# Two large graph aggregations: waits placed on small memsets instead of register operations, sizes loaded as 16-bit values, the last one's tiles in a loop

## The chip, the core and the metric

The kernel runs on one core of a Trainium2 chip. The metric is the device time of one execution in microseconds. Engines: PE (TensorE), DVE (VectorE), ACT (ScalarE), POOL (GpSimd) and SP (SyncE).
## The reference

Two graph layers, each followed by a mixture of experts, on 6250 nodes of 256 features. The change touches the two full-width graph attention layers, which compute for each node d over its edges (s, d), some 206250 of them:

```python
e = leaky_relu(e_left[src] + e_right[dst], 0.2)
e_exp = exp(e - segment_max(e, dst)[dst])
alpha = e_exp / (segment_sum(e_exp, dst)[dst] + EPS)
out = segment_sum(Wh[src] * alpha[:, :, None], dst)
```

The first layer has 8 heads of 32 channels, the last 4 heads of 64 (with roles of source and destination swapped and no self loops). Between them stands a small attention layer of 4 heads of 4 channels, which has a function of its own (`aggregate_small`) and is not touched.

## The kernel before

Edges are sorted by destination on the chip and nodes ranked by degree, so that 128 nodes with similar degrees form a tile (NT = 49 tiles). A list gives each of the 128 partitions its neighbours, slot by slot. `aggregate` runs one large aggregation; it is called twice, for the first layer (with 8 heads, and `beside` holding pieces of the sorting of the other two lists, which DVE, PE and ACT do between tiles) and for the last (4 heads, nothing beside).

- **POOL** (`Stream.gpsimd`, L902 to L915) gathers rows of the table by indirect DMA, one slot of 128 rows per instruction (L914), into a ring of 96 slots. It waits at L906 on `taken`, which DVE raises, before it overwrites ring entries of 16 slots.
- **SP** (`Stream.sync`) waits for gathers, raises `ready` and loads index lists.
- **ACT** (`lay`, L1129 to L1148) waits for `ready`, copies the scores' left parts out of the ring into `el` in groups of 16 slots (L1142) and blanks the edges of the chunk (L1145, L1146); `tile` (L1151) takes the exponential (L1155) and lays the next chunk, and stores the tile's result (L1127).
- **DVE** (`tile`, L1047 to L1109) does the rest. A tile's slots are cut into chunks of up to 64 slots; here nearly every tile is one chunk. Per chunk it makes the scores and the running maximum (L1055 to L1067), waits for the exponential, multiplies the tail's eight slots into `wide` (L1070, recorded at L1042), and then runs a register loop over units of eight slots (L1075): product into `part` (recorded at L1042), sum into `wide` (L1080). It folds `wide` and adds it to `acc` (L1081 to L1095). At a tile's end it divides and writes `res` (L1100 to L1108).

Sizes of a tile (number of slots per chunk, chunks, first slot, first chunk) stand in `sizes` and are loaded into registers by L1006. The loops over chunks and units are loops of the sequencer; the loop over tiles is written out 49 times.
## Time and profile before

| | us |
|---|---|
| median of three runs (lowest, highest) | 10115.43 (10109.69, 10125.95) |
| span of the profiled execution | 10110.4 |
| DVE busy | 5594.3 (55%) |
| POOL busy | 5337.1 (53%) |
| PE busy | 2288.8 (23%) |
| ACT busy | 1093.7 (11%) |

The profiled execution's own time is its span. Register, branch, wait and DMA-issuing instructions are not counted as busy; where they are shown they carry a q after the engine's name (DVEq). In a timeline a row gives the start, the duration, the engine, the line and in brackets the engine's idle time before it and what ended it; "issue" is time for which the profile knows no other cause. In a group row the numbers are busy time in all, the mean duration of one in ns, and the idle time before them with its releasers. The first large aggregation lies between about 1063 and 3690 us, the last between about 6383 and 8751 us.

### The profile page before, as it was taken

How to read it: one execution, taken by the hardware profiler on the slowest of the kernel's cores; microseconds unless marked ns; L12 is line 12 of the kernel's file. 1: busy time of each engine (PE TensorE's matmuls, PEld its weight loads, DVE VectorE, ACT ScalarE, POOL GpSimd, SP SyncE). 2: the span in 40 equal slices, each digit the busy share in tenths (PEclk: the TensorE clock that was granted, in tenths of full speed). 3: DMA queues.
4: the chain of work that ended last, by engine and by line, in shares of the span. 5: the costliest groups of instructions: out<-in, count | busy, mean ns of one | idle time of the engine just before them, and what ended most of it. 6: DMA issues, size and time to landing. Idle time of an engine off the chain costs nothing. (4 is left out here: it accounts for less than half of the span.)

```text
span 10110.4 us, 54577 instructions
## 1 busy us (share of the span) xinstructions
PE 2288.8 (23%) x9111; PEld 1752.0 (17%) x9112; DVE 5594.3 (55%) x8828; ACT 1093.7 (11%) x2533; POOL 5337.1 (53%) x5411
## 2 busy tenths in 40 slices
PE   2112000000000002146555512000000000129995
PEld 1111000000000001135444411000000000116663
DVE  8764588788777677523333275455656556421111
ACT  1101000000000001112222201000000000002221
POOL 0025656666676654455555345776666777542221
PEclk7555555555555555578777755555555555559997
DMA  4051333433333353411111162433333333620004
GB/s 142 22 159 50 97 82 87 122 99 98 101 101 98 102 113 74 122 23 33 29 28 28 30 172 89 109 100 92 101 98 101 106 99 99 129 97 30 30 30 117
DMA packets 458121, 869.43 MB, mean 86 GB/s; under 512 B 175134, under 2 KB 294860, under 8 KB 448192
## 3 DMA queue, kind: packets, MB, share of 16 engines
q0 software_dynamic: 239536, 575.99, 23.0%
q1 hardware_dynamic: 167648, 182.04, 6.2%
q10 hardware_dynamic: 50788, 110.02, 3.3%
q14 instruction: 129, 1.06, 0.0%
q8 instruction: 20, 0.33, 0.0%
HBM read 693.35 MB, written 180.71 MB: 86 GB/s over the span
## 5 line engine op out<-in xcount | busy, mean ns | idle before, releaser
L914 POOL DMA_INDIRECT agg_ring<-table,agg_idx x4320 | 4275.8, 990 | 2329.8 <-issue 1323.4
L1042 DVE TENSOR_TENSOR agg_part<-agg_ring,agg_prob 128x2048 f32 x420 | 964.4, 2296 | 631.8 <-issue 556.2
L1080 DVE TENSOR_TENSOR agg_wide<-agg_wide,agg_part 128x2048 f32<-128x2048 f32 x420 | 960.4, 2287 | 14.4
L1786 PE MATMUL dense_tp<-all_ident,dense_xn 128*128 128x128 f32 x100 | 23.9, 425 | 2570.3 <-issue 2543.7
L1408 PE MATMUL agg_hp<-agg_xt,agg_w 128*128 128x256 f32 x1600 | 446.4, 439 | 579.4 <-ACT agg_ht L1378 340.3
L2208 DVE TENSOR_TENSOR experts_h<-experts_sg,experts_hp 128x682 f32<-128x682 f32 x106 | 91.8, 866 | 779.7 <-ACT experts_sg L2191 779.7
L2158 PE MATMUL experts_hp<-mixture_w,experts_xt 128*128 x1696 | 518.2, 458 | 0.6 <-ACT experts_xt L2187 0.6
L1408 PEld LDWEIGHTS agg_hp<-agg_xt,agg_w 128*128 128x128 f32 x1600 | 352.4, 224 | 663.8 <-ACT agg_ht L1378 360.4
L1786 PEld LDWEIGHTS dense_tp<-all_ident,dense_xn 128*128 128x128 f32 x100 | 20.3, 228 | 2571.9 <-issue 2544.5
L2129 POOL DMA_INDIRECT yc<-experts_ysb,experts_list x105 | 103.7, 987 | 685.2 <-DVE experts_ysb L2217 685.2
L1422 PE MATMUL agg_yp<-agg_w,agg_ht 128*128 128x256 f32 x1600 | 405.3, 411 | 231.0 <-remote 174.5
L1422 PEld LDWEIGHTS agg_yp<-agg_w,agg_ht 128*128 128x128 f32 x1600 | 330.4, 208 | 297.1 <-issue 246.9
L1042 DVE TENSOR_TENSOR agg_wide<-agg_ring,agg_prob 128x2048 f32 x98 | 224.2, 2288 | 275.0 <-issue 198.8
L488 POOL IOTA rank_thresholds<- 128x50 int32 x3 | 0.5, 170 | 686.4 <-POOLq L75 686.4
L2158 PEld LDWEIGHTS experts_hp<-mixture_w,experts_xt 128*128 128x128 f32 x1696 | 314.4, 190 | 174.6 <-issue 30.0
L217 PE MATMUL agg_words_turned<-all_ident,last_sort_words 128*128 128x128 f32 x48 | 10.9, 416 | 1454.1 <-issue 1454.1
L2179 PE MATMUL experts_yp<-mixture_w,experts_ht 128*128 x1260 | 309.4, 387 | 0.0
L1155 ACT ACTIVATE agg_prob<-agg_score 128x648 f32<-128x648 f32 (+1 forms) x98 | 56.7, 579 | 2332.1 <-issue 1387.9
L1055 DVE TENSOR_TENSOR agg_score<-agg_el,agg_er 128x640 f32<-128x640 f32 (+1 forms) x98 | 64.6, 659 | 410.0 <-issue 372.4
L514 POOL DMA_INDIRECT rank_start_g<-starts,rank_node_i x147 | 143.3, 975 | 225.9 <-DVE rank_degt L625 182.0
L217 PEld LDWEIGHTS agg_words_turned<-all_ident,last_sort_words 128*128 128x128 f32 x48 | 8.8, 216 | 1456.4 <-issue 1456.0
L522 POOL DMA_INDIRECT rank_wide<-copies,rank_widx x147 | 148.9, 1013 | 195.6 <-DVE rank_widx L679 154.8
(421 smaller groups left out, 6520.8 us busy)
## 6 DMA issues: line engine op xcount, KB each, us to landing
agg_ring<-table,agg_idx POOLq DMA_INDIRECT x4320
y<-agg_ysb ACTq DMA_DIRECT2D x25, 1024.0 KB
rank_y<-y SPq DMA_DIRECT2D x10, 2560.0 KB
rank_x<-x SPq DMA_DIRECT2D x30, 640.0 KB
copies<-first_sort_words SPq DMA_DIRECT2D x16, 1024.0 KB
copies<-last_sort_words ACTq DMA_DIRECT2D x16, 1024.0 KB
x<-rank_x SPq DMA_DIRECT2D x20, 640.0 KB
agg<-agg_res ACTq DMA_DIRECT2D x98, 128.0 KB
```

The costliest lines, as they stand in the source:

```text
L514: pool.indirect_dma_start(out=start_g[:, t:t + 1], out_offset=None, in_=starts.rearrange("(n a) -> n a", a=1), in_offset=bass.IndirectOffs ...
L522: pool.indirect_dma_start(out=wide[g % 2][:, u * ROW:(u + 1) * ROW], out_offset=None, in_=copies.rearrange("c (r w) -> (c r) w", w=ROW), i ...
L914: pool.indirect_dma_start(out=self.ring[:, to:to + self.RW], out_offset=None, in_=self.table, in_offset=bass.IndirectOffsetOnAxis(ap=index ...
L1042: return dve.tensor_tensor(to[:, :].rearrange("p (j h c) -> p j h c", j=UNIT, h=H), ring[:, ds(st.at(at_u), UNIT * RW)].rearrange("p (j w) ...
L1055: dve.tensor_tensor(sc3, el3, er[:, H:2 * H].unsqueeze(1).to_broadcast([P, SC // H, H]), ALU.add).then_inc(added, 1)
L1080: dve.tensor_tensor(wide[:, :], wide[:, :], part[:, :], ALU.add).then_inc(widened, 1)
L1408: mm = pe.matmul(self.hp[:, h:h + 2 * P], self.w1[:, at:at + P], xt3[:, :, k * P:(k + 1) * P], start=(k == 0), stop=(k == 1))
L1422: mm = pe.matmul(y, self.ht[:, n * 2 * P + u * P:n * 2 * P + (u + 1) * P], self.w2[:, n * D:(n + 1) * D], start=(c == 0), stop=(c == 3))
L2129: pool.indirect_dma_start(out=yc, in_=ysb[t % B][:, :], in_offset=None, out_offset=bass.IndirectOffsetOnAxis(ap=lst[:, t * 4 + 1:t * 4 + 2 ...
L2158: mm = pe.matmul(hp3[:, c, 0:HC], xt[:, kc * P:(kc + 1) * P], rhs, start=(kc == 0), stop=(kc == 1))
L2179: mm = pe.matmul(yp[:, 0:D], ht[0:m, j * P:(j + 1) * P], w2[0:m, ds(e * W2 + j * D, D)], start=(j == 0), stop=(j == HJ - 1))
L2208: dve.tensor_tensor(h[:, :].rearrange("p (c n) -> p c n", c=2), sg[:, :].rearrange("p (c n) -> p c n", c=2), hp3[:, 2:4, 0:HC], ALU.mult). ...
```

## The change

In `aggregate` alone. On DVE the waits for the exponential, the tail, the previous sum, the end of a chunk and the store of the result each get a memset of one to seven elements behind them (`passed`), so that the memset carries the wait; on ACT small activations into `junk` take the waits for `ready` and `copied`. Addresses and bounds are computed ahead of the waits and kept (`snap`). The event instructions that raised `dve_passed` go. The first slot of a tile is held as two 16-bit values, high part and low four bits, and the load takes six 16-bit values instead of five 32-bit ones. The position in `prob` is counted from the even unit at or below the first (`even`). Shifts and masks are written as divisions and remainders. WIDE is 16, as SLOTS is, so the groups have the size they had. Where nothing stands beside the aggregation (the last one) DVE's tiles 1 to 48 are a loop of the sequencer instead of being written out.

```diff
--- before.py
+++ after.py
@@ -971,6 +971,10 @@
 EARLY = 112
 
 
+LOAD = 6
+WIDE = 16
+
+
 def aggregate(nc, cfg, H, C, table, info, ell, out, self_loop, S, beside):
 
 
@@ -979,33 +983,36 @@
     CW = H * C
     RW = CW + 2 * H
     UH, UC = UNIT * H, UNIT * CW
-    GH = SLOTS * H
-    SC = (CH // SLOTS + 1) * GH
+    GH = WIDE * H
+    SC = (CH // WIDE + 1) * GH
+    WU = WIDE // UNIT
     with Scope(nc, f"agg{cfg.name}", S["keep"]) as s:
         st = Stream(nc, s, cfg, RW, table, ell, info)
         ring, taken = st.ring, st.taken
-        sizes = s.sb("sizes", [1, 5 * (NT + 1)], I32)
+        sizes = s.sb("sizes", [1, LOAD * (NT + 1)], mybir.dt.uint16)
+        bits = s.sb("bits", [1, 2 * (NT + 1)], I32)
...
         def sizes_of(eng, t):
             why = "the ranking bounds every size of a tile"
-            ng, nk, c0, k0, missing = nc.values_load_multi_w_load_instructions(sizes[0:1, ds(t * 5, 5)], engines=[eng.engine], min_val=0, max_val=cfg.max_slots,
-                                                                      skip_runtime_bounds_check_because=why)[1]
-            return nc.s_assert_within(ng, 1, CH, skip_runtime_bounds_check_because=why), nk, c0, k0, missing
+            ng, nk, c_high, c_low, k0, missing = nc.values_load_multi_w_load_instructions(
+                sizes[0:1, ds(t * LOAD, LOAD)], engines=[eng.engine], min_val=0, max_val=cfg.max_slots, skip_runtime_bounds_check_because=why)[1]
+            return nc.s_assert_within(ng, 1, CH, skip_runtime_bounds_check_because=why), nk, c_high * SLOTS + c_low, k0, missing
 
...
@@ -1025,32 +1032,39 @@
                 dve.wait_ge(st.info_in, 16)
-                of_tile = sizes[:, :].rearrange("p (t w) -> p t w", w=5)
+                of_tile = sizes[:, :].rearrange("p (t w) -> p t w", w=LOAD)
+                bits2 = bits[:, :].rearrange("p (t w) -> p t w", w=2)
+                dve.tensor_scalar(bits2[:, :, 0], st.inf[:, I_C0:I_C0 + NT + 1], 4, None, ALU.logical_shift_right).then_inc(halved, 1)
+                dve.tensor_scalar(bits2[:, :, 1], st.inf[:, I_C0:I_C0 + NT + 1], SLOTS - 1, None, ALU.bitwise_and).then_inc(halved, 1)
                 dve.tensor_scalar(of_tile[:, :, 0], st.inf[:, I_NG:I_NG + NT + 1], 1.0, None, ALU.max).then_inc(sized, 1)
-                dve.tensor_scalar(of_tile[:, :, 4], st.inf[:, I_NK:I_NK + NT + 1], -1.0, 4096.0, ALU.mult, ALU.add).then_inc(sized, 1)
-                for w, first in ((1, I_NK), (2, I_C0), (3, I_K0)):
-                    dve.tensor_copy(of_tile[:, :, w], st.inf[:, first:first + NT + 1]).then_inc(sized, 1)
+                dve.tensor_copy(of_tile[:, :, 1], st.inf[:, I_NK:I_NK + NT + 1]).then_inc(sized, 1)
+                dve.tensor_copy(of_tile[:, :, 4], st.inf[:, I_K0:I_K0 + NT + 1]).then_inc(sized, 1)
+                dve.tensor_scalar(of_tile[:, :, 5], st.inf[:, I_NK:I_NK + NT + 1], -1.0, 4096.0, ALU.mult, ALU.add).then_inc(sized, 1)
+                dve.wait_ge(halved, 2)
+                dve.tensor_copy(of_tile[:, :, 2:4], bits2[:, :, :]).then_inc(sized, 1)
                 dve.wait_ge(const, 5)
                 dve.wait_ge(sized, 5)
                 dve.sem_inc(taken, cfg.RU - 1)
                 dve.sem_inc(widened, cfg.RU)
                 acc3 = acc[:, :].rearrange("p (h c) -> p h c", h=H)
+                res3 = res[:, :].rearrange("p (h c) -> p h c", h=H)
                 sc3 = score[:, 0:SC].rearrange("p (j h) -> p j h", h=H)
                 el3 = el[:, GH:GH + SC].rearrange("p (j h) -> p j h", h=H)
 
-                def weigh(at_u, u, to):
-                    return dve.tensor_tensor(to[:, :].rearrange("p (j h c) -> p j h c", j=UNIT, h=H),
-                                             ring[:, ds(st.at(at_u), UNIT * RW)].rearrange("p (j w) -> p j w", w=RW)[:, :, 0:CW].rearrange("p j (h c) -> p j h c", h=H),
+                def weigh(at, to, u):
+                    return dve.tensor_tensor(to, ring[:, ds(at, UNIT * RW)].rearrange("p (j w) -> p j w", w=RW)[:, :, 0:CW].rearrange("p j (h c) -> p j h c", h=H),
                                              prob[:, ds(u * UH, UH)].rearrange("p (j h) -> p j h", h=H).unsqueeze(3).to_broadcast([P, UNIT, H, C]),
                                              ALU.mult)
 
-                def tile(t):
+                def tile(t, later):
                     ng, nk, c0, k0, _ = sizes_of(dve, t)
                     with dve.Fori(0, nk) as k:
-                        gg = c0 + k * ng
                         kk = dve.snap(k0 + k + 1)
-                        u0, u1 = gg >> 3, (gg + ng) >> 3
-                        nu = st.units(u1 - u0)
+                        gg = dve.snap(c0 + k * ng)
+                        u0, u1 = dve.snap(gg // UNIT), dve.snap((gg + ng) // UNIT)
+                        even = dve.snap(u0 // WU * WU)
+                        ending = dve.snap(st.at(u1))
+                        in_prob = nc.s_assert_within(u1 - even, 0, CU + WU - 2, skip_runtime_bounds_check_because="a chunk has 8 to 64 slots")
                         dve.wait_ge(laid, kk * 3)
                         dve.tensor_tensor(sc3, el3, er[:, H:2 * H].unsqueeze(1).to_broadcast([P, SC // H, H]), ALU.add).then_inc(added, 1)
                         dve.wait_ge(added, kk)
@@ -1066,16 +1080,16 @@
                         dve.wait_ge(kept, kk)
                         dve.tensor_tensor(sc3, sc3, mn[:, :].unsqueeze(1).to_broadcast([P, SC // H, H]), ALU.subtract).then_inc(scored, 1)
                         dve.wait_ge(probs, kk)
-                        first = u0 & 1
-                        weigh(u1, nu + first, wide).then_inc(tail, 1)
-                        n0 = dve.snap(u0 + cfg.RU)
-                        n1 = dve.snap(u1 + cfg.RU)
+                        dve.memset(passed[:, 5:6], 0.0)
+                        weigh(ending, wide[:, :].rearrange("p (j h c) -> p j h c", j=UNIT, h=H), in_prob).then_inc(tail, 1)
                         dve.wait_ge(tail, kk)
-                        dve.sem_inc(st.dve_passed, 1)
+                        dve.memset(passed[:, 0:1], 0.0)
+                        n0, n1 = dve.snap(u0 + cfg.RU), dve.snap(u1 + cfg.RU)
                         with dve.Fori(n0, n1) as n:
-                            u = nc.s_assert_within(n - n0, 0, CU - 2, skip_runtime_bounds_check_because="a chunk has 8 to 64 slots")
+                            u = nc.s_assert_within(n - even - cfg.RU, 0, CU - 1, skip_runtime_bounds_check_because="a chunk has 8 to 64 slots")
                             dve.wait_ge(widened, n)
-                            weigh(n, u + first, part).then_inc(taken, 1)
+                            dve.memset(passed[:, 6:7], 0.0)
+                            weigh(st.at(n), part[:, :].rearrange("p (j h c) -> p j h c", j=UNIT, h=H), u).then_inc(taken, 1)
                             dve.wait_ge(taken, n)
                             dve.tensor_tensor(wide[:, :], wide[:, :], part[:, :], ALU.add).then_inc(widened, 1)
                         dve.tensor_reduce(dsum[:, :], prob[:, 0:SC].rearrange("p (j h) -> p h j", h=H), AX.X, ALU.add).then_inc(totalled, 1)
@@ -1086,30 +1100,37 @@
                         dve.wait_ge(widened, n1)
                         dve.tensor_tensor(wide[:, 0:4 * CW], wide[:, 0:4 * CW], wide[:, 4 * CW:8 * CW], ALU.add).then_inc(quartered, 1)
                         dve.wait_ge(quartered, kk)
...
+                        dve.wait_ge(dens, kk)
+                        dve.memset(passed[:, 1:2], 0.0)
                         dve.wait_ge(combined, kk)
-                        dve.wait_ge(dens, kk)
-                        dve.sem_inc(st.dve_passed, 1)
-                    beside.vector(dve, t)
+                        dve.memset(passed[:, 2:3], 0.0)
+                    if beside.parts:
+                        beside.vector(dve, t)
                     dve.memset(m[:, :], NEG).then_inc(reset, 1)
                     dve.wait_ge(reset, t + 1)
                     dve.tensor_scalar(den[:, :], den[:, :], 1e-16, None, ALU.add if self_loop else ALU.max).then_inc(floored, 1)
                     dve.wait_ge(floored, t + 1)
-                    dve.reciprocal(den[:, :], den[:, :]).then_inc(inverted, 1)
-                    dve.wait_ge(inverted, t + 1)
-                    if t:
+                    dve.reciprocal(den[:, :], den[:, :]).then_inc(parts_done, 1)
+                    if later:
                         dve.wait_ge(out_stored, t * 16)
-                    dve.tensor_tensor(res[:, :].rearrange("p (h c) -> p h c", h=H), acc3,
-                                      den[:, :].unsqueeze(2).to_broadcast([P, H, C]), ALU.mult).then_inc(tile_done, 1)
-
-                for t in range(NT):
-                    tile(t)
+                        dve.memset(passed[:, 3:4], 0.0)
+                    dve.wait_ge(parts_done, t + 1)
+                    dve.tensor_tensor(res3, acc3, den[:, :].unsqueeze(2).to_broadcast([P, H, C]), ALU.mult).then_inc(tile_done, 1)
+
+                tile(0, False)
+                if beside.parts:
+                    for t in range(1, NT):
+                        tile(t, True)
+                else:
+                    with dve.Fori(1, NT) as t:
+                        tile(t, True)
 
             @block.tensor
             def _(pe):
@@ -1128,22 +1149,27 @@
 
                 def lay(t, fresh, k):
                     ng, nk, c0, k0, missing = sizes_of(act, t)
-                    gg = c0 + k * ng
+                    gg = act.snap(c0 + k * ng)
                     kk = k0 + k + 1
-                    g0, g1 = gg >> 4, (gg + ng) >> 4
-                    at = gg & (SLOTS - 1)
+                    g0, g1 = act.snap(gg // WIDE), act.snap((gg + ng) // WIDE)
+                    at = act.snap(gg % WIDE)
                     shown = at if self_loop else at + fresh
                     to = fresh * H
-                    act.wait_ge(st.ready, g1 + 1)
-                    act.activation(er[:, ds(to, H)], ring[:, ds((gg % cfg.RS) * RW + CW + H, H)], ACT.Copy).then_inc(laid, 1)
-                    act.activation(junk[:, :], zeros[:, 0:1], ACT.Exp)
-                    groups = nc.s_assert_within(g1 - g0 + 1, 1, CH // SLOTS + 1, skip_runtime_bounds_check_because="a chunk has up to 64 slots")
-                    with act.Fori(0, groups) as g:
-                        act.activation(el[:, ds((g + 1) * GH, GH)].rearrange("p (j h) -> p j h", h=H),
-                                       ring[:, ds(((g0 + g) % cfg.RING) * (SLOTS * RW), SLOTS * RW)].rearrange("p (j w) -> p j w", w=RW)[:, :, CW:CW + H], ACT.Copy).then_inc(copied, 1)
-                    act.wait_ge(copied, g1 + kk)
-                    act.activation(el[:, ds(shown * H, GH)], negs[:, 0:GH], ACT.Copy).then_inc(laid, 1)
-                    act.activation(el[:, ds((at + ng + SLOTS) * H, SC)], negs[:, :], ACT.Copy).then_inc(laid, 1)
+                    end = act.snap(g1 + 1)
+                    ready = act.snap(end * (WIDE // SLOTS))
+                    mine = act.snap((gg % cfg.RS) * RW + CW + H)
+                    act.wait_ge(st.ready, ready)
+                    act.activation(junk[:, 0:1], zeros[:, 0:1], ACT.Exp)
+                    act.activation(er[:, ds(to, H)], ring[:, ds(mine, H)], ACT.Copy).then_inc(laid, 1)
+                    with act.Fori(g0, end) as g:
+                        place = nc.s_assert_within(g - g0 + 1, 1, CH // WIDE + 1, skip_runtime_bounds_check_because="a chunk has up to 64 slots")
+                        act.activation(el[:, ds(place * GH, GH)].rearrange("p (j h) -> p j h", h=H),
+                                       ring[:, ds((g % (cfg.RS // WIDE)) * (WIDE * RW), WIDE * RW)].rearrange("p (j w) -> p j w", w=RW)[:, :, CW:CW + H], ACT.Copy).then_inc(copied, 1)
+                    before, behind, all_copied = act.snap(shown * H), act.snap((at + ng + WIDE) * H), act.snap(g1 + kk)
+                    act.wait_ge(copied, all_copied)
+                    act.activation(junk[0:1, 1:2], zeros[0:1, 0:1], ACT.Copy)
+                    act.activation(el[:, ds(before, GH)], negs[:, 0:GH], ACT.Copy).then_inc(laid, 1)
+                    act.activation(el[:, ds(behind, SC)], negs[:, :], ACT.Copy).then_inc(laid, 1)
 
                     return nk, k0, missing
 
@@ -1153,8 +1179,8 @@
                     with act.Fori(0, nk) as k:
                         act.wait_ge(scored, k0 + k + 1)
                         act.activation(prob[:, 0:SC + H], score[:, 0:SC + H], ACT.Exp).then_inc(probs, 1)
-                        fresh = act.snap(nc.s_assert_within((k + missing + 1) >> 12, 0, 1, skip_runtime_bounds_check_because="k is below the number of chunks"))
-                        following = lay(nc.s_assert_within(fresh + t, 0, NT, skip_runtime_bounds_check_because="the next tile"), fresh, (k + 1) * ((fresh + 1) & 1))
+                        fresh = act.snap(nc.s_assert_within((k + missing + 1) // 4096, 0, 1, skip_runtime_bounds_check_because="k is below the number of chunks"))
+                        following = lay(nc.s_assert_within(fresh + t, 0, NT, skip_runtime_bounds_check_because="the next tile"), fresh, (k + 1) * ((fresh + 1) % 2))
                     beside.scalar(nc, act, t)
                     return following
 
```

## Rows read from the trace of the kernel before

**Rows 1.** The page: busy us, share of the span, instructions of each engine.
```profile
PE 2288.8 (23%) x9111; PEld 1752.0 (17%) x9112; DVE 5594.3 (55%) x8828; ACT 1093.7 (11%) x2533; POOL 5337.1 (53%) x5411
```

**Rows 2.** Both stretches: span; PE, PEld, DVE, ACT, POOL busy; PE clock, DMA.
```profile
1120.00:3690.00 2570.00, 49.97 (x208) 39.87 (x208) 1971.59 (x2093) 172.92 (x443) 1642.07 (x1652) 0.50 0.37 96
6400.00:8750.00 2350.00, 0.00 (x0) 0.00 (x0) 1410.35 (x1365) 108.58 (x390) 1672.45 (x1663) 0.50 0.39 99
```

**Rows 3.** POOL's waits for DVE, 6800 to 7800 us (total us, times, longest us).
```profile
POOL agg_ring L914 <- DVE agg_part L1042: 116.9, 23, 8.2
```

**Rows 4.** Groups, 1120 to 3690 us (busy, mean ns, idle before, its releasers).
```profile
L914 POOL DMA_INDIRECT agg_ring<-table,agg_idx x1645 | 1638.5, 996 | 891.1 <-issue 506.3 <-DVE agg_part L1042 384.7
...
L1042 DVE TENSOR_TENSOR agg_part<-agg_ring,agg_prob 128x2048 f32 x208 | 477.7, 2297 | 139.2 <-issue 74.2 <-DVE agg_wide L1080 50.1 <-DVE agg_wide L1042 14.9
...
L1042 DVE TENSOR_TENSOR agg_wide<-agg_ring,agg_prob 128x2048 f32 x48 | 109.8, 2288 | 118.9 <-ACT agg_prob L1155 61.5 <-issue 57.4
...
L1055 DVE TENSOR_TENSOR agg_score<-agg_el,agg_er 128x640 f32<-128x640 f32 x48 | 39.6, 825 | 70.7 <-issue 43.1 <-ACT agg_el L1146 27.6
...
L1083 DVE TENSOR_TENSOR agg_den<-agg_den,agg_prob 128x8 f32<-128x8 f32 x48 | 7.9, 164 | 1.6
...
L1100 DVE MEMSET agg_m<- 128x8 f32 x49 | 3.2, 65 | 0.0
```

**Rows 5.** Groups, 6400 to 8750 us: the gathers and the unit's product.
```profile
L914 POOL DMA_INDIRECT agg_ring<-table,agg_idx x1663 | 1673.3, 1006 | 662.0 <-issue 515.7 <-DVE agg_part L1042 146.2
L1042 DVE TENSOR_TENSOR agg_part<-agg_ring,agg_prob 128x2048 f32 x208 | 477.6, 2296 | 490.3 <-issue 480.4 <-DVE agg_wide L1080 5.4 <-DVE agg_wide L1042 4.5
```

**Rows 6.** DVE's timeline in the first aggregation (start, us, [idle before]).
```profile
2490.48 2.29 DVE L1042 TENSOR_TENSOR agg_wide<-agg_ring,agg_prob 128x2048 f32 x1 [1.52 <-issue]
2493.51 2.30 DVE L1042 TENSOR_TENSOR agg_part<-agg_ring,agg_prob 128x2048 f32 x1 [0.74 <-issue]
...
2498.57 2.30 DVE L1042 TENSOR_TENSOR agg_part<-agg_ring,agg_prob 128x2048 f32 x1 [0.44 <-issue]
```

**Rows 7.** ACT's exponential in the first aggregation, from ACT's timeline.
```profile
2147.07 0.71 ACT L1155 ACTIVATE agg_prob<-agg_score 128x648 f32<-128x648 f32 x1 [34.39 <-issue]
```

**Rows 8.** DVE's timeline from one tile to the next, first aggregation.
```profile
1592.04 0.42 DVE L1108 TENSOR_TENSOR agg_res<-agg_acc,agg_den 128x256 f32<-128x256 f32 x1
1593.47 0.83 DVE L1055 TENSOR_TENSOR agg_score<-agg_el,agg_er 128x640 f32<-128x640 f32 x1 [1.01 <-issue]
```

**Rows 9.** DVE's timeline, a tile of four units, last aggregation.
```profile
7001.00 0.43 DVE L1108 TENSOR_TENSOR agg_res<-agg_acc,agg_den 128x256 f32<-128x256 f32 x1
...
7019.08 2.29 DVE L1042 TENSOR_TENSOR agg_part<-agg_ring,agg_prob 128x2048 f32 x1 [4.74 <-issue]
...
7026.08 2.29 DVE L1042 TENSOR_TENSOR agg_part<-agg_ring,agg_prob 128x2048 f32 x1 [2.38 <-issue]
...
7048.73 0.43 DVE L1108 TENSOR_TENSOR agg_res<-agg_acc,agg_den 128x256 f32<-128x256 f32 x1
```

**Rows 10.** DVE's timeline, a tile of five units, last aggregation.
```profile
8206.81 0.42 DVE L1108 TENSOR_TENSOR agg_res<-agg_acc,agg_den 128x256 f32<-128x256 f32 x1
...
8261.30 0.42 DVE L1108 TENSOR_TENSOR agg_res<-agg_acc,agg_den 128x256 f32<-128x256 f32 x1 [0.44 <-issue]
```

**Rows 11.** DVE's timeline, a tile of four units that ran freely.
```profile
7277.16 0.43 DVE L1108 TENSOR_TENSOR agg_res<-agg_acc,agg_den 128x256 f32<-128x256 f32 x1
...
7310.37 0.42 DVE L1108 TENSOR_TENSOR agg_res<-agg_acc,agg_den 128x256 f32<-128x256 f32 x1
```

**Rows 12.** Line 1075, 2000 to 2900, then 6800 to 7200 us (min/median/max ns).
```profile
L1075 DVEq COMPARE_BRANCH  x78: 50/56/375, 2013.7 to 2878.7; - x78
...
L1075 DVEq COMPARE_BRANCH  x33: 4/700/1396, 6806.4 to 7181.7; - x33
```

**Rows 13.** DVE's timeline after a burst of sort instructions.
```profile
2537.67 0.20 DVE L1104 RECIPROCAL agg_den<-agg_den 128x8 f32<-128x8 f32 x1 [1.89 <-remote]
2539.07 0.42 DVE L1108 TENSOR_TENSOR agg_res<-agg_acc,agg_den 128x256 f32<-128x256 f32 x1 [1.20 <-DVE agg_den L1104]
```

27 lines of the change are left out of this document (14 added, 13 removed).

## The prediction

> **What bounds the kernel now.** The page first [rows 1]: VectorE (DVE) is busy 55% of the span and GpSimd (POOL) 53%, so neither is the limit of the whole, and the change touches only the two large aggregations. So I cut out their stretches [rows 2]: 1120 to 3690 us and 6400 to 8750 us, 4920 us together. POOL issues about 1650 gathers in each. A gather costs its own duration, about 1.0 us, and 0.3 us of issue (506.3 us over 1645 gathers) [rows 4, 5]; that is 1.30 us, or 2144 us for the first stretch's 1645 and 2189 us for the last's 1663. The rest is POOL waiting for DVE to give ring entries back: 384.7 us in the first, 146.2 us in the last [rows 4, 5]. These two waits are all that a faster DVE can win here. In the middle of the last aggregation they are thick, 116.9 us of 1000 [rows 3]; outside it little is left, so the last one is balanced between POOL and DVE, and the first is DVE's.
>
> What does DVE do between its instructions? In the first aggregation it idles 0.44 us before every product of a unit but the first of its chunk (0.74 us there), and 1.52 us before the product of the tail, of which the exponential on ACT takes 0.71 [rows 6, 7]; between two tiles 1.01 us [rows 8]. A wait that stands on an engine instruction costs 0.03 us (line 1083: 1.6 us over 48) [rows 4]. The difference is what a wait on a register instruction costs: DVE's sequencer sits on it, and only then computes the addresses of the next product.
>
> In the last aggregation the same code is slower. A unit, with the same two 2.29 us instructions, recurs after 7.00 us [rows 9], although nothing that the trace knows is waited for: 480.4 of 490.3 us of idle time are "issue" [rows 5]. Line 1075's branch, 56 ns in the middle of the first aggregation, is 700 ns here [rows 12]. In the kernel's list of instructions a unit has five that the sequencer executes itself (a move, three fused register instructions, a branch), so each stands for 1.40 us. A whole tile has 14 + 5U of them, U being its units (three at the tile's edge; 1 + 4 + 1 + 1 before the units; 1 + 1 + 2 behind). For U = 4 this gives 34 x 1.40 = 47.6 us, and the rows show 47.73 [rows 9]; for U = 5, 39 x 1.40 = 54.6 against 54.49 [rows 10]. The count alone explains the tile, so the 28 or 30 engine instructions cost the sequencer nothing visible, and its waits nothing either. A tile of four units can run in 33.21 us when this pacing is off [rows 11].
>
> **The change, part by part.**
>
> *Waits on memsets, first aggregation.* The sequencer now runs ahead of the engine; a memset with a wait costs 0.03 us for the wait, 0.065 us of its own [rows 4] and 0.03 us behind: 0.13 us. Per product behind a sum: 0.44 - 0.13 = 0.31 us, x 160 (208 units less 48 first ones) = 50 us. First product of a chunk: the tail's wait and the unit's, two memsets, 0.74 - 0.23 = 0.5 us, x 48 = 25 us. Tail: 1.52 - 0.71 - 0.13 = 0.68 us, x 48 = 33 us. Tile edge: the wait for the store moves to a memset, so the load of sizes (six 16-bit values for five of 32 bits) lies under earlier work: 1.01 - 0.1, x 48 = 44 us. Chunk end: one event wait becomes two memsets, nothing within 0.1 us x 48. Sum 152 us of DVE time. POOL also waits for what the change leaves: ACT's copies and late exponentials (61.5 and 27.6 us in [rows 4]). And after a burst of sort instructions small DVE instructions too come only 1.4 us apart (2537.67 to 2539.07) [rows 13]; three or four memsets more in such a place cost up to 5 us in a tile. If a third of the 48 tiles have it fully, that is 16 x 5 = 80 us at most; I take half of it, 40, and 110 of the 152 us remain. Bounds: 152 us above; below, nothing.
>
> *Last aggregation, same edits.* Here the count decides. Removed from the sequencer per chunk: the event wait behind the tail and the one at the end; the other waits stood on instructions that stay, since their arithmetic stays. The arithmetic is regrouped: 19 operations in five instructions become about 21 (the split of c0 into two halves, the even start), in groups of up to seven, so again four or five. Per chunk that is 11 + 5U before, about 8 + 5U after. The unit itself keeps nine address operations in two instructions, a move, an increment and a branch: five, 7.0 us. Removed per tile: the event wait for the store.
>
> *The tile loop, last aggregation only.* It adds the address of the sizes, t + 1, 16t, the increment and the branch: five; the load and the move stay. A tile's edge goes from 3 to 7. Together 15 + 5U for 14 + 5U: one more, 1.4 us per paced tile. About 40 of the 48 are paced: +56 us, less where POOL is the limit; I take +45. The memsets, 5 + U per tile, I cost at nothing here, because 28 engine instructions cost nothing now; their cover is the sequencer's slowness, and if it goes they cost 0.13 us each. Bounds for the count: three fewer to three more per tile, -130 us (then POOL's 146 us are nearly used up) to +190 us (4.2 us x 45).
>
> By the count of rows that is the sum. The Trainium skill (Advanced Engine Details and Errata, Control Flow Timing) gives a compare-and-branch about 108 ns. By that, five instructions of a unit hide under its 4.6 us of arithmetic and the last aggregation would be free of the pacing, as the free tile is; the 700 ns row speaks against it for this stretch.
>
> *16-bit sizes, WIDE in place of SLOTS (both 16), ACT's edits.* ACT lays the next chunk under DVE's units; 0.
>
> Sum: -110 + 45 = -65 us on the profiled 10110.4 us, which stands 5 us (0.05%) under the runs' median of 10115.43. So 10050 us.
>
> **The rivals.**
>
> *Run-ahead pays in both.* The pacing of the last aggregation ends, because no register instruction waits any more. For: the free tile [rows 11]; DVE then needs some 30 to 38 us per tile and POOL, at 1.30 us x 35 gathers, 45. Against: its tiles are explained by a count, with no waits in it. Gain: 110 + 146 = 256, 9860 us. The skill (Perfetto Trace Analysis, DVE / Act Engine Instruction) says that an engine instruction waits in a queue beside the sequencer, which goes on decoding; that is this rival's mechanism.
>
> *The loop's registers cost more (slower).* Place: DVE's sequencer in the last aggregation's paced tiles. If the edge and the snapshots add four instead of one (t copied, t + 1 and 16t not shared, the early snapshots split over more instructions), a tile costs 5.6 us more, x 45 = 250 us, less 110: 10255 us; with three, 10195. It decides from 110 / 45 / 1.4 = 1.7 instructions more per tile. For: the regrouping is my estimate. Against: three event waits are surely gone.
>
> *Memsets are paced too (slower).* If each costs 1.4 us of a separate stream, a tile has 25 + 3U engine instructions against 15 + 5U of the sequencer: with 208 units over 48 tiles, 38.0 x 1.4 = 53.2 us against 49.9 before, x 44 = +145 us; and the first aggregation loses its gain. 10260 us. For: [rows 13]. Against: the last aggregation's engine instructions show no spacing now. It turns the sum at 65 / 905 memsets = 0.07 us each.
>
> *Nothing moves.* DVE's 152 us become waits for ACT or a landing, or the last aggregation gives back what the first wins: 10110 us. For: ACT is late by 61.5 us already. Against: 384.7 us of POOL's wait name DVE.
>
> **How the numbers follow.** Forecast 10050 us, chance 0.42; run-ahead in both 0.15; loop registers 0.16; memsets paced 0.12; nothing moves 0.15. About 0.2% (20 us) is what a measurement of this kernel can tell from no change. Faster: 0.42 + 0.15, less 0.03 of the forecast's spread that lies within 20 us, 0.54. Same: that 0.03 and 0.11 of the last rival, 0.14. Slower: 0.16 + 0.12 and 0.04 of the last rival, 0.32. The range goes from 9900, which takes in half of the first rival, to 10230, which holds the loop rival at three instructions and leaves the other slower one out. The faster cases' own range is 9860 to 10090.
>
> **What would show it.** In the first aggregation: 0.13 us of idle time before a product instead of 0.44, tile edges near 0.1 us, POOL's wait for DVE about 270 us instead of 385, the stretch 110 us shorter. In the last: units still 7.0 us apart, tiles of four units near 49 us. Wrong if units there come closer than 6 us (first rival), if tiles grow by 4 us or more with units at 7.0 (loop registers), or if units grow beyond 7.0 us and small instructions stand 1.4 us apart (memsets paced).

## The result and the profile after

The changed kernel takes **10201.0 us** (median of 4 runs, 10187.86 to 10208.55) against 10120.69 us for the kernel before in the same session: ratio 1.0076, 95% interval 1.0062 to 1.009. It is slower. The forecast was 10050 us and faster; the measured time lies inside the range (9900 to 10230), but above the kernel before instead of below it.

The page of the changed kernel, beside [rows 1] (its line numbers: 1055 is the product of a unit and of the tail, formerly 1042; 1094 the sum, formerly 1080; 1125 the result of a tile, formerly 1108; 1083, 1086, 1091, 1111, 1113 and 1123 are the memsets that carry waits):

```profile
span 10194.2 us, 55246 instructions
...
PE 2292.0 (22%) x9111; PEld 1752.8 (17%) x9112; DVE 5642.9 (55%) x9740; ACT 1123.3 (11%) x2633; POOL 5265.4 (52%) x5411
```

DVE has 912 instructions more and is 49 us busier, mostly the memsets at 59 ns each. The groups of the first aggregation, 1140 to 3720 us, answer to [rows 4] (busy, mean ns, idle before, releasers; 1083 is the memset in front of the tail's product, 1091 the one in front of a unit's):

```profile
L914 POOL DMA_INDIRECT agg_ring<-table,agg_idx x1629 | 1623.3, 996 | 931.5 <-issue 501.3 <-DVE agg_part L1055 430.3
L1055 DVE TENSOR_TENSOR agg_part<-agg_ring,agg_prob 128x2048 f32 x208 | 477.6, 2296 | 68.0 <-issue 68.0
L1094 DVE TENSOR_TENSOR agg_wide<-agg_wide,agg_part 128x2048 f32<-128x2048 f32 x208 | 475.6, 2287 | 15.7 <-DVE agg_part L1055 8.9
L1055 DVE TENSOR_TENSOR agg_wide<-agg_ring,agg_prob 128x2048 f32 x48 | 109.8, 2288 | 30.5 <-issue 30.5
L1069 DVE TENSOR_TENSOR agg_score<-agg_el,agg_er 128x640 f32<-128x640 f32 x47 | 39.3, 836 | 91.1 <-issue 63.5 <-ACT agg_el L1172 27.7
L1091 DVE MEMSET agg_passed<- 1x1 f32 x208 | 12.3, 59 | 17.7 <-issue 8.9
L1083 DVE MEMSET agg_passed<- 1x1 f32 x48 | 2.8, 59 | 79.4 <-ACT agg_prob L1181 64.4 <-issue 14.9
```

Read alone, the products look like the gain that was forecast: 68.0 us of idle time before them for 139.2, 30.5 for 118.9 before the tail. But before the tail nearly all of it only moved to the memset in front (79.4 us), and before the units the memsets take back about half (17.7 us of idle time and 12.3 us of their own). The row that counts is the first: POOL, whose gathers set when the stage ends, waits 430.3 us for DVE and not 385 or the 270 of the forecast.

Where the 84 us between the two profiled spans arise, by the starts of the tiles' results: the first aggregation, from its first result (1131.1 us before, 1137.4 after) to its 49th (3676.0, 3721.4), is 2544.9 us before and 2584.1 after, **+39**; the stages between, whose code is the same, +21; the last, from result to result (6383.8 to 8751.0 before, 6450.3 to 8833.2 after), 2367.2 before and 2382.9 after, **+16**; some 8 at the two ends. In two more profiles of the changed kernel the first aggregation is +30 and +65, the last +10 and +8, and the middle -11 and +27, so the middle's share is not the change's.

**Units and tiles after.** DVE's timeline of a tile of four units in the last aggregation, beside [rows 9] (start, us, [idle before]):

```profile
7022.58 0.43 DVE L1125 TENSOR_TENSOR agg_res<-agg_acc,agg_den 128x256 f32<-128x256 f32 x1 [1.22 <-issue]
...
7028.18 0.71 DVE L1073 TENSOR_REDUCE agg_bm<-agg_score 128x4 f32<-128x320 f32 x1 [0.91 <-DVE agg_score L1071]
7029.58 0.16 DVE L1075 TENSOR_TENSOR agg_mn<-agg_m,agg_bm 128x4 f32<-128x4 f32 x1 [0.69 <-DVE agg_bm L1073]
7030.98 0.16 DVE L1077 TENSOR_TENSOR agg_score<-agg_m,agg_mn 128x4 f32<-128x4 f32 x1 [1.24 <-DVE agg_mn L1075]
7032.38 0.17 DVE L1079 COPY agg_m<-agg_mn 128x4 f32<-128x4 f32 x1 [1.24 <-DVE agg_score L1077]
...
7066.08 0.06 DVE L1111 MEMSET agg_passed<- 1x1 f32 x1 [0.98 <-remote]
7067.48 0.06 DVE L1113 MEMSET agg_passed<- 1x1 f32 x1 [1.34 <-remote]
...
7074.46 0.43 DVE L1125 TENSOR_TENSOR agg_res<-agg_acc,agg_den 128x256 f32<-128x256 f32 x1 [1.22 <-DVE agg_den L1120]
```

Instructions of 0.06 to 0.71 us start 1.40 us apart, and the tile takes 51.88 us. It has 37 engine instructions: 37 x 1.40 = 51.8. In the kernel before the same stretch showed this pace on the sequencer's instructions ([rows 12]: the branch of 700 ns), 34 of them, 47.7 us. The sequencer of the changed kernel has 35 in such a tile. The branch is now, in the same stretch of 6800 to 7200 us (min/median/max ns):

```profile
L1088 DVEq COMPARE_BRANCH  x37: 50/56/185, 6801.1 to 7195.6; - x37
```

So the pace did not go; it sits on the longer of two streams, and the memsets, 5 + U per tile, made the engine's the longer one in tiles of four units. Not every tile is paced throughout. Of the 24 tiles of four units in the last aggregation, 17 are within 0.8 us of 34 x 1.40 before and 11 within 0.8 us of 37 x 1.40 after; the rest are mostly shorter, and the mean of all 24 even fell, from 46.3 to 45.4 us.

The first aggregation suffers in the tiles with sort work behind the chunk. Before, a tile from 2483.62 to 2539.07 us; after, its counterpart from 2498.74 to 2569.99, 71.3 for 55.5 us:

```profile
2498.74 0.49 DVE L1125 TENSOR_TENSOR agg_res<-agg_acc,agg_den 128x256 f32<-128x256 f32 x1
...
2549.69 2.54 DVE L197 TENSOR_TENSOR last_sort_words<-last_sort_words 128x512 f32<-128x512 f32 x4 [4.97 <-remote]
2555.29 2.56 DVE L197 TENSOR_TENSOR last_sort_words<-last_sort_words 128x512 f32<-128x512 f32 x4 [3.06 <-remote]
2560.19 2.54 DVE L197 TENSOR_TENSOR last_sort_words<-last_sort_words 128x512 f32<-128x512 f32 x4 [2.34 <-remote]
2562.68 0.07 DVE L1116 MEMSET agg_m<- 128x8 f32 x1
2567.19 0.17 DVE L1118 TENSOR_SCALAR agg_den<-agg_den 128x8 f32<-128x8 f32 x1 [4.45 <-issue]
...
2569.99 0.42 DVE L1125 TENSOR_TENSOR agg_res<-agg_acc,agg_den 128x256 f32<-128x256 f32 x1 [1.20 <-DVE agg_den L1120]
```

It holds 53 engine instructions where the one before held 44. The stalls do not sit at the memsets but at whatever comes when the run of quick instructions has gone on for some time: "remote" and "issue" are what the trace puts down where it knows no reason. This tile grew the most. Together with five others, it holds the loss: the tiles that start at 2279, 2484, 2586, 2738, 3050 and 3285 us in the kernel before are 52 us longer in this profile, 41 and 64 us in the two other profiles of the changed kernel. All other tiles together lie between 13 us shorter and 2 us longer.

### The profile page after: what moved, and what is told of

Read it like the earlier page. It is cut to its first block and busy times, and to the rows that moved or that the text cites. A ratio compares the mean times of both kernels' runs of the same rounds, so it can differ in the third digit from the quotient of the medians.

```text
span 10194.2 us, 55246 instructions
## 1 busy us (share of the span) xinstructions
PE 2292.0 (22%) x9111; PEld 1752.8 (17%) x9112; DVE 5642.9 (55%) x9740; ACT 1123.3 (11%) x2633; POOL 5265.4 (52%) x5411
## 5 line engine op out<-in xcount | busy, mean ns | idle before, releaser
L914 POOL DMA_INDIRECT agg_ring<-table,agg_idx x4320 | 4202.7, 973 | 2487.7 <-issue 1315.1
L506 POOL DMA_INDIRECT rank_row<-words,rank_qi x150 | 151.1, 1007 | 195.8 <-DVE rank_junk L593 92.0
```

What stands on the lines that cost most here:

```text
L506: pool.indirect_dma_start(out=row[i % 2][:, v * COARSE:(v + 1) * COARSE], out_offset=None, in_=rows, in_offset=bass.IndirectOffsetOnAxis(a ...
L914: pool.indirect_dma_start(out=self.ring[:, to:to + self.RW], out_offset=None, in_=self.table, in_offset=bass.IndirectOffsetOnAxis(ap=index ...
```

## The experiments

**Two conditions.** The experiments ran on seven chips, and the kernel before does not take the same time on them: near 10120 us on three (the condition of the prediction, whose own chip is not on record; below, *with the pace*) and near 9118 us on four (*without it*). Within a session both kernels run on one chip, so each ratio is sound, but it belongs to its condition. Why chips differ is not shown; the runs only show what differs. Without the pace DVE's own instructions never come 1.40 us apart more than once in a row, and in the last aggregation nineteen gathers of twenty recur after 1.25 us. (In the first one, short runs of some ten gathers at 1.40 us stand in both conditions, from about 1340 to 1930 us.)

**1. Double the unit's memset.**

```
     dve.memset(passed[:, 6:7], 0.0)
+    dve.memset(passed[:, 4:5], 0.0)
```

> The changed kernel (10201 us) with a second empty memset per unit (208 more in each large aggregation). Theory A, in the last aggregation VectorE's own instructions are spaced at least 1.40 us on average, whatever they are: a tile of four units has 41 of them instead of 37, so 57.4 us instead of 51.8; 1.4 x 208 x 0.85 = +245 us there and up to +60 in the late part of the first aggregation, 10400 to 10510 us. Theory B, a memset costs what its row shows (0.06 us and 0.03 to 0.07 around it) and the loss came from elsewhere: +20 to +60 us. Theory C, one common pace for engine and sequencer instructions together (72 in 51.8 us, 0.72 us each): a tile grows by 2.9 us, +125 us.

> A second memset per unit, once more. If the kernel before is near 10115 in this call (the paced condition): theory A as before, tiles of four units in the last aggregation at 57.4 us instead of 51.8, ratio to the kernel before 1.020 to 1.038; theory B 1.009 to 1.013; theory C (one pace for both kinds) 1.015 to 1.022. If it is near 9116: ratio 0.999 to 1.001 again, from all.

Without the pace: 9114.86 us, ratio 0.9999 (0.9989 to 1.0008); the change with 416 memsets more costs nothing measurable. With it: 10213.49 us, ratio 1.0115 (1.0078 to 1.0152). DVE's timeline with the pace, one tile of four units:

```profile
6961.96 0.42 DVE L1126 TENSOR_TENSOR agg_res<-agg_acc,agg_den 128x256 f32<-128x256 f32 x1 [1.21 <-issue]
...
7019.37 0.42 DVE L1126 TENSOR_TENSOR agg_res<-agg_acc,agg_den 128x256 f32<-128x256 f32 x1 [1.22 <-issue]
```

57.41 us with 41 engine instructions: 41 x 1.40 = 57.4, as theory A had it. The total did not follow: +245 us were expected in the last aggregation, and the stretch is 2422.1 us, 39 to 47 more than in the three profiles of the changed kernel. The paced tiles, 7 of the 24 of four units, alternate with free ones (33.8 us for four units at 6805 and 33.9 at 7063). The first aggregation, 2579.5 us, lies among the changed kernel's (2575.2 to 2610.2): the six tiles named above are 88 us longer than before instead of 41 to 64, and the others are shorter by as much. By total time the second memset cannot be told from none: on the same chip, in another session, the changed kernel stands at 1.0091 (1.0073 to 1.011). So the ratio lies in the range given for theory B while the tile is A's: A had the tile right and the sum wrong, and the ratio alone would have misled. What the memsets cost altogether is seen in experiment 2, and what carries the stretch in experiment 3.

**2. Take the memsets out.** The five of a chunk's loop are left out; their waits stand on register and event instructions again, all else stays as changed.

```
     dve.wait_ge(probs, kk)
-    dve.memset(passed[:, 5:6], 0.0)
...
-    dve.memset(passed[:, 0:1], 0.0)
...
-    dve.memset(passed[:, 6:7], 0.0)
...
-    dve.memset(passed[:, 1:2], 0.0)
...
-    dve.memset(passed[:, 2:3], 0.0)
```

> The changed kernel with the five empty memsets of a chunk's loop taken out (5:6, 0:1, 6:7, 1:2, 2:3), their waits on register and event instructions again as before the change; tile loop, 16-bit sizes, regrouped arithmetic and ACT's edits stay. If the kernel before is near 10115 (paced): theory A (the nine memsets of a tile are what costs, above all in the first aggregation's tiles with sort work, where VectorE's own instructions come 1.40 us apart in places): ratio to the kernel before 0.998 to 1.002. Theory B (the loss lies in the other parts): 1.005 to 1.009 as for the changed kernel. If it is near 9116 (no pace): 0.999 to 1.002 from both.

> The five memsets of a chunk's loop taken out, once more, for the paced condition, which the last call did not have. If the kernel before is near 10115: theory A (nine memsets a tile are what costs there): ratio to the kernel before 0.999 to 1.003, clearly under the changed kernel's 1.006 to 1.008. Theory B (the other parts of the change cost it: they cost 0.26% without any pace, too): 1.005 to 1.009. If it is near 9116: 1.0026 again.

With the pace: 10153.38 us, ratio **1.0014** (1.0003 to 1.0025). The changed kernel gave 1.0076, and 1.0062 and 1.0091 in other sessions (it did not run in this one), so the memsets are 0.5 to 0.8% of it there, most of the loss. The first aggregation is 2535.7 us long, 9 less than before where the changed kernel has 30 to 65 more, and the six tiles that held its loss are back at their old length (1 us shorter in sum). Line 1055's register instructions are back at the pace (6800 to 7200 us):

```profile
L1055 DVEq FUSED_REGOPS  x102: 3/690/1399, 6803.0 to 7194.8; - x102
```

Tiles of four units have 36 of the sequencer's instructions here and take 50.4 us (36 x 1.40). Without the pace: 9139.13 us, 1.0026 (1.0016 to 1.0037). There the memsets are worth having, since the kernels that keep them stand at 0.9999 (two_unit_memsets, with the tile loop, and experiment 5, without it). They differ from this one in the last aggregation (2155.4 us against 2126.4 and 2130.6), not in the first (2369.1 against 2372.1 and 2371.3); why, where POOL is the bound, stays open.

**3. Let the working instructions wait.** The unit's product alone, first with the wait on the register instruction, then on the product itself:

```
-    dve.wait_ge(widened, n)
-    dve.memset(passed[:, 6:7], 0.0)
-    weigh(st.at(n), part[...], u).then_inc(taken, 1)
+    weigh(st.at(n), part[...], u)._wait_ge(widened, dve.to_reg(n)).then_inc(taken, 1)
```

> The changed kernel without the unit's memset; the wait stands on the register instruction again, all else as changed. Theory A: a tile of four units in the last aggregation has 33 engine instructions (46.2 us) and 35 sequencer instructions (49.0 us), so it falls from 51.8 to 49.0 us, the branch's 0.70 us rows come back, and the time falls by 80 to 130 us to 10070 to 10120; in undisturbed tiles of the first aggregation nothing changes by more than 0.1 us per unit. Theory B: -10 to -25 us, 10180. Theory C: 68 x 0.72 = 49.0 us per tile, like A in time, but the branch's rows stay short.

> The changed kernel without the unit's memset and with the wait on the product itself, its address instructions ahead of the wait. Theory A with the sequencer at most one instruction ahead of the engine: the addresses are now worked out under the sum, so the idle time before a product behind a sum falls from 0.38 to 0.03 us (208 x 0.35 = 70 us in each aggregation of DVE time), and a tile of four units in the last aggregation has 33 engine and 31 sequencer instructions: 46.2 us instead of 51.8. 9950 to 10030 us. Theory B: 0.13 us per unit and no more, 10150. Rival D, the register instructions cost the same wherever they stand (a product's start waits for them in any case): 10070 to 10120 as with the wait on the register instruction.

> The wait on the unit's product itself, no unit memset, once more. Paced: theory A: 208 memsets fewer in each large aggregation and the product's addresses under the sum; 0.995 to 1.000, between the changed kernel (1.007) and the one with all waits on work (0.9925). Rival, only the position counts and memsets are free: 0.997 too in an unpaced call, so it is the distance from no_memsets that tells: more than 0.004 under it speaks for position, less for the count. No pace: 0.996 again.

All three fell on chips without the pace: wait_on_register 9127.07 us, 1.0012 (1.0002 to 1.0021); wait_on_product 9078.53, **0.9961** (0.9947 to 0.9975), and 9075.16, 0.9959. So moving the wait behind the address instructions gives 0.5%, with no memset at the unit in either. The edit also saves the sequencer one instruction a unit; that it is the position that counts is read from the rows. What the pace makes of this edit by itself was not seen. The reason can be read around one product. The changed kernel (with the pace, but in an undisturbed tile), where the sum began at 2069.58:

```profile
2069.58 2.29 DVE L1094 TENSOR_TENSOR agg_wide<-agg_wide,agg_part 128x2048 f32<-128x2048 f32 x1
2071.92 0.06 DVE L1091 MEMSET agg_passed<- 1x1 f32 x1
2072.29 2.30 DVE L1055 TENSOR_TENSOR agg_part<-agg_ring,agg_prob 128x2048 f32 x1 [0.32 <-issue]
```

and the register instructions in front of that product (min/median/max ns, first and last start):

```profile
L1055 DVEq FUSED_REGOPS  x2: 57/148/240, 2071.9 to 2072.2; - x2
```

They start with the memset, at 2071.9, and not under the sum: the sequencer hands the waiting memset over and takes nothing up behind it until it has started. The memset took the wait's place and hid nothing; from the sum's end to the product it is 0.42 us for 0.44 before. With the wait on the product (wait_on_product_b):

```profile
2035.17 2.29 DVE L1092 TENSOR_TENSOR agg_wide<-agg_wide,agg_part 128x2048 f32<-128x2048 f32 x1
2037.49 2.30 DVE L1055 TENSOR_TENSOR agg_part<-agg_ring,agg_prob 128x2048 f32 x1
```

```profile
L1055 DVEq FUSED_REGOPS  x1: 57/57/57, 2035.8 to 2035.8; - x1
```

The last of them now starts at 2035.8, under the sum that began at 2035.17, and the product follows after 0.035 us. Over 160 products behind a sum that is 0.39 x 160 = 62 us of DVE's idle time; the first aggregation fell by 44 us, from 2371.3 us (experiment 5's kernel) to 2327.4.

Then the same for the tail, and fewer waits in all: the tail's product waits for `probs` itself and increments `widened`, the unit's product waits for `n + kk` of it, and the denominator's wait is folded into `folded`; two of the six memsets are left (the expectations miscount them as five of seven gone; it is four of six).

```
-    dve.memset(passed[:, 5:6], 0.0)
-    weigh(ending, wide[...], in_prob).then_inc(tail, 1)
-    dve.wait_ge(tail, kk)
-    dve.memset(passed[:, 0:1], 0.0)
+    chunk = dve.to_reg(kk)
+    weigh(ending, wide[...], in_prob)._wait_ge(probs, chunk).then_inc(widened, 1)
...
+    summed = dve.to_reg(dve.snap(n + kk))
+    weigh(st.at(n), part[...], u)._wait_ge(widened, summed).then_inc(taken, 1)
...
-    dve.wait_ge(dens, kk)
-    dve.memset(passed[:, 1:2], 0.0)
```

> The changed kernel with five of its seven memsets gone: the waits of the tail's product and of the unit's product stand on the products themselves, the tail is counted in the sum's semaphore, the wait for the denominator is folded into the one before the accumulator. Theory A: a tile of four units has 30 engine and some 31 sequencer instructions, 43.4 us against 51.8, and GpSimd's 35 gathers of about 1.26 us (44 us) become the bound of the last aggregation; both aggregations together 280 to 380 us shorter, 9820 to 9920 us, clearly under the kernel before. Theory B: some 11 memsets per tile at 0.1 us, 96 tiles, -100 us at most, 10100. Rival D: 10000 to 10060.

> Five memsets gone, waits on the products themselves, once more. If the kernel before is near 10115 (the paced condition): theory A: tiles of four units in the last aggregation have 30 engine and 32 sequencer instructions, so 44.8 us instead of 51.8 (before 47.7), and the first aggregation loses its idle time before products: ratio to the kernel before 0.965 to 0.985. Theory B: 0.998 or more. If it is near 9116: 0.992 again.

Without the pace 9037.19 us, **0.9917** (0.9901 to 0.9934); with it 10025.38, **0.9925** (0.99 to 0.995). It beats both kernels in both conditions, by less than A's 0.965 to 0.985. With the pace the gain is in the first aggregation, 2468.6 us for 2544.9; the last has 2358.8 for 2367.2. Tiles of four units take 44.8 us (32 sequencer instructions x 1.40; 30 engine instructions). But such a tile also has 32 gathers, so its length alone does not tell whether DVE or POOL sets it. POOL, 6400 to 8600 us, and its timeline:

```profile
L914 POOL DMA_INDIRECT agg_ring<-table,agg_idx x1578 | 1696.5, 1075 | 504.2 <-issue 503.9 <-DVE agg_part L1055 0.3
```

```profile
7001.08 1.09 POOL L914 DMA_INDIRECT agg_ring<-table,agg_idx  x1 [0.31 <-issue]
7002.47 1.09 POOL L914 DMA_INDIRECT agg_ring<-table,agg_idx  x1 [0.30 <-issue]
7003.87 1.10 POOL L914 DMA_INDIRECT agg_ring<-table,agg_idx  x1 [0.30 <-issue]
```

It no longer waits for DVE (0.3 us), and a gather takes 1.40 us on average: (1696.5 + 504.2) / 1578 = 1.395. Between the first and the last result, 56% of them start 1.38 to 1.42 us apart and 32% 1.25; without the pace it is 1.25 for 95% of them in the same kernel. **The gathers are under the pace themselves.** 1675 of them at 1.40 are 2345 us, and the last aggregation was 2367 before: by this estimate only some 22 us were to be had there, whatever DVE does, and 8 came. When POOL is held up often, it runs free in between: of its gathers in the last aggregation 68% start 1.25 us apart in the kernel before, and 94% in the changed one and with two memsets a unit. So it gives most of a DVE delay back, which would explain why the second memset costs the stretch some 40 us and not 245. This last step is read from traces, and no run varied it by itself.

**4. The other parts of the change.** The kernel before with 16-bit sizes only (six values, of which two are combined, for five of 32 bits), the changed kernel with ACT's part as before, and the changed kernel beside them.

```
-    ng, nk, c0, k0, missing = nc.values_load_multi_w_load_instructions(sizes[0:1, ds(t * 5, 5)], ...)[1]
+    ng, nk, c_high, c_low, k0, missing = nc.values_load_multi_w_load_instructions(
+        sizes[0:1, ds(t * LOAD, LOAD)], ...)[1]
```

> The kernel before with only its sizes changed (six 16-bit values per tile, two of them combined, for five of 32 bits), nothing else of the change. Theory E, the load at a tile's edge takes longer (1.39 to 1.45 us in the changed kernel for 0.6 to 1.2) and each load is on the sequencer's path at an edge: +0.3 to 0.8 us for 48 tiles of the first aggregation, +15 to +30 us, ratio 1.0015 to 1.003 without the pace; with it the same within its noise. Rival F, the load costs nothing and what is left of the change's cost sits in ACT's edits: 1.000.

> The kernel before with 16-bit sizes only, once more. Without the pace, theory E: 1.002 to 1.003, that is what is left of no_memsets (1.0026); rival: 1.000, and the regrouped arithmetic carries it. With the pace: 1.0021 again within 0.001.

> The changed kernel with ACT's part written as in the kernel before (no snapshots, no waiting activation, ring address in place of the wide index). Theory E: ACT lays the next chunk under VectorE's units, so nothing changes: the ratio of the changed kernel in the same call, within 0.001. Rival F: 0.002 to 0.003 under it.

> The changed kernel in the same call, for comparison: 0.999 to 1.001 if the kernel before is near 9116, 1.006 to 1.008 if it is near 10115.

> The changed kernel as it is, once more, beside the kernel before. In the last four runs the kernel before took 9116 us and not 10120, and no stretch of them shows instructions 1.40 us apart. Theory A (the 1.40 us per VectorE instruction is what made the changed kernel lose; it is a condition of the chip, absent here): if the kernel before is again near 9116, the changed one is equal to it or up to 20 us faster (a product behind a sum starts 0.38 us after it in both, the second memset of a unit cost nothing), ratio 0.998 to 1.001; if it is near 10120, the ratio is 1.005 to 1.010 again. Theory B (the loss lies in what the change does to the tile loop, the loads or ACT, and not in that pace): the ratio is 1.005 to 1.010 in both cases.

With the pace: sizes_only 10157.31 us, 1.0021 (1.001 to 1.0031); act_before 10234.22, 1.0101 (1.0078 to 1.0124); the changed kernel 10226.3, 1.0091 (1.0073 to 1.011), and in another session 10168.16, 1.0062 (1.0046 to 1.0079). Without it: sizes_only_b 9142.43, **1.0029** (1.0017 to 1.004). That is near the 1.0026 of no_memsets, but by stretches not the same loss: sizes_only_b has 2384.9 and 2138.3 us in the two aggregations, no_memsets 2369.1 and 2155.4. ACT's edits are worth nothing that can be told (1.0101 without them, 1.0091 with them, and the intervals overlap; tried with the pace alone). The load at the tile's edge in the first aggregation, before (with the pace) and with 16-bit sizes (sizes_only_b, without it):

```profile
L1006 DVEq TENSOR_LOAD <-agg_sizes x48: 585/1191/3483, 1131.1 to 3589.1; - x48
```

```profile
L1010 DVEq TENSOR_LOAD <-agg_sizes x48: 1385/1500/4106, 1070.7 to 3365.5; - x48
```

On average 1.09 us before and 1.60 there (1.58 in sizes_only, with the pace); 0.5 x 48 = 24 us, about what sizes_only costs (0.21% of 10131 us are 21, 0.29% of 9118 us are 26). With the pace 15 us of it lie in the first aggregation (2559.9 us for 2544.9).

**5. The tile loop undone.**

```
-                if beside.parts:
+                if True:
                     for t in range(1, NT):
                         tile(t, True)
```

> The changed kernel with the last aggregation's tiles written out again instead of looped. Paced: theory A: the sequencer has three or four instructions fewer per tile, but the memsets make the other stream the longer one, and GpSimd's own 1.40 us per gather bounds the stretch: no change from the changed kernel, ratio to the kernel before 1.005 to 1.009. Rival, the loop's registers cost 1.4 us per tile and more: 0.999 to 1.003. No pace: 1.000 within 0.001.

9115.05 us, 0.9999 (0.999 to 1.0008), without the pace. It is also the closest there is to the changed kernel in that condition, with the same first aggregation; the changed kernel itself never ran on such a chip, and the loop's cost with the pace was not measured. It adds five sequencer instructions a tile (35 for 30 with four units). With four units the sequencer's stream is still the shorter one, 35 instructions against the engine's 37; with five units the two have 40 each, and with six it is the longer (45 against 43), so there a cost of the loop with the pace is not excluded.

**6. The load under the sum.** waits_on_work, tiles written out, with the next tile's sizes loaded behind the units' loop:

```
+    following = sizes_of(dve, t + 1)
     dve.tensor_reduce(dsum[:, :], prob[:, 0:SC]...
...
-    ng, nk, c0, k0, _ = sizes_of(dve, t)
+    ng, nk, c0, k0, _ = sizes_now
```

> waits_on_work with the sizes of the next tile loaded behind the last sum of the units (written out, no tile loop) instead of at the tile's edge. Theory: the sequencer runs at most one instruction ahead of the engine, so a load of 1.39 to 1.45 us at the edge, under a result of 0.49, leaves 1.2 us of idle time per tile, and behind the 2.29 us sum it is covered: 48 x 1.2 = 58 us of VectorE's time in the first aggregation, where VectorE is the bound; nothing in the last, where GpSimd is. Ratio to the kernel before 0.985 to 0.989 without the pace (waits_on_work 0.9917), 0.986 to 0.992 with it (0.9925). Rival: ACT or a landing is late next and the edge's time goes there: no change from waits_on_work.

> The version with the next tile's sizes loaded behind the last sum, once more, for the condition with the 1.40 us pace. If the kernel before is near 10115: theory: the first aggregation gains 58 us more than waits_on_work (0.9925) where its tiles are not paced, the last one nothing, since GpSimd's gathers at 1.40 us bound it: ratio 0.986 to 0.991. Rival, the edge's time is given back to the pace in the same stretch: 0.992 to 0.994. If it is near 9116: 0.987 again.

> The same kernel, a last time, still for the condition with the 1.40 us pace. Kernel before near 10115: theory 0.986 to 0.991, rival 0.992 to 0.994. Near 9116: 0.987 again, and it stays open whether it beats waits_on_work under the pace.

All three runs were without the pace: 9000.68 us, **0.9871** (0.9856 to 0.9886), 9004.87 and 0.9873, 8998.02 and 0.987. The load takes 1.39 us, from 2028.5 on, under the last sum:

```profile
2028.36 2.29 DVE L1090 TENSOR_TENSOR agg_wide<-agg_wide,agg_part 128x2048 f32<-128x2048 f32 x1
...
2045.95 0.48 DVE L1120 TENSOR_TENSOR agg_res<-agg_acc,agg_den 128x256 f32<-128x256 f32 x1
2046.35 0.81 DVE L1069 TENSOR_TENSOR agg_score<-agg_el,agg_er 128x640 f32<-128x640 f32 x1
```

The idle time at the edge, 1.41 us in waits_on_work (median), is gone; the first aggregation is 2252.9 us for 2293.3 in waits_on_work, 40 us of the 58 expected. Whether it keeps its lead over waits_on_work with the pace stays open.

## Why the prediction was wrong

**The sum in the first aggregation (-110 us) failed at "the sequencer now runs ahead of the engine".** It gave 0.31 us per product behind a sum. The register instructions in front of the product start when the memset starts and not before, so the product follows the sum after 0.42 us instead of 0.44: 3 us over 160 products for the 50 that were summed. The same holds for the first product of a chunk (0.75 us before, 0.68 after, medians, where the forecast had 0.23; two memsets at its own 0.13 would have been 0.26) and for the tail. In the fifteen tiles from 1342 to 2090 us, where DVE's pace does not show, the forecast's 152 us over 48 tiles would have been 47 us less; the changed kernel is 3 to 6 us longer there in its three profiles. Where the addresses do run ahead, with the wait on the product, the idle time is 0.035 us (and the same fifteen tiles are 24 us shorter in waits_on_work_b); the mechanism exists and the change does not use it. The Trainium skill (Perfetto Trace Analysis, DVE / Act Engine Instruction) has the sequencer go on decoding while an engine instruction waits in its queue; behind an instruction that waits, these rows do not agree: nothing was taken up there before it had started.

**"The memsets ... I cost at nothing here, because 28 engine instructions cost nothing now"** is the other failing step. They cost nothing only while the sequencer's 34 were the longer stream. Paced tiles of four units:

| kernel | engine | sequencer | longer x 1.40 | tile, us |
|---|---|---|---|---|
| before | 28 | 34 | 47.6 | 47.7 |
| changed | 37 | 35 | 51.8 | 51.9 |
| two memsets a unit | 41 | 35 | 57.4 | 57.4 |
| no memsets | 29 | 36 | 50.4 | 50.4 |
| waits on work | 30 | 32 | 44.8 | 44.8 |

The count itself was right: 35 sequencer instructions were forecast for the changed tile of four units, and 35 there are. The rival "memsets are paced too", given 0.12, is what came, with its 25 + 3U engine instructions (37 for U = 4) exact. It was given no place in the range, so that the range holds 10201 us is luck. It was priced at +145 us in the last aggregation, which showed +8 to +16, and at nothing gained in the first, which lost 30 to 65. Its total, 10260, is 59 us above the measurement, but both of its terms were off.

**The last aggregation's +45 us** was +16, although a paced tile grew by 4.2 us and not by 1.4. What the prediction lacked is POOL: it took 1.30 us a gather as fixed and 146 us as POOL's reserve. The 1.30 is a mean: in the kernel before most of these gathers are 1.25 us apart and a fifth 1.40. With the pace gathers that are not held up come 1.40 us apart on average, so most of that wait was never to be had, and lost time is largely given back.

**Where the first aggregation's loss comes from**: [rows 13] had been read rightly, small engine instructions 1.40 us apart behind a burst, and charged with 40 us, half of an upper bound. That term was mis-sized: by no_memsets_b (-9 us) and the changed kernel (+30 to +65) the memsets cost 39 to 74 us there, with no 152 us of gain to set against them.

**The size load** was put under earlier work, 44 us of gain from [rows 8]. It became longer (1.09 to 1.57 us on average) and stayed where it was, and the idle time before the next tile's scores rose from 70.7 to 91.1 us. This alone is 0.2 to 0.3%. That it stays for the same reason as the addresses is not shown by itself.

ACT's edits at 0 were right. The rival "run-ahead pays in both" did not occur: there was no run-ahead, and in waits_on_work, which has it, the pace stayed all the same. "Nothing moves" missed the loss, though giving back is what the last aggregation does. And "loop registers cost more" did not occur, since the sequencer had its 35 instructions and no more.

## What to carry to other kernels

A wait that must not hold up address arithmetic belongs on the working instruction, with the registers computed ahead of it; an empty instruction in between moves the wait and hides nothing, because the sequencer here stays one instruction behind whatever waits. Before adding "free" small instructions, count both streams of the engine (its own and the sequencer's) and also what the engine that waits for it can really do: a reserve read off a wait is not all there. And time such a change on more than one chip: this one is 0.6 to 0.9% slower on some, and its nearest relatives are equal to the kernel before on others.
